# Two fused attention and feed-forward layers: the second layer's norms, projections and row-maximum tiles in another order

## The reference

```python
xn = layernorm(x)
x = x + linear_attention(xn) + ternary_silu_ffn(xn)          # layer 0
xn = layernorm(x)
q, k, v = rope(xn @ q_w.T + q_b), rope(xn @ k_w.T + k_b), xn @ v_w.T + v_b   # 16 heads of 16
attn = softmax(q @ k.T / 4) @ v                              # 1024 x 1024 per head and batch
x = x + attn @ out_w.T + out_b + hadamard_ffn(xn)            # layer 1, hidden size 1024
```

## Time and profile before

| | |
|---|---|
| median of three runs | 838.94 us |
| the profiled execution's own time | 838.99 us |
| its span | 837.2 us |
| busy in the span | PE 762.6 (91%), DVE 533.3 (64%), ACT 430.1 (51%), POOL 290.6 (35%) |
| the stage of layer 1's feed-forward network | 256.40 to 519.75 us, 263.35 us |

### The profile page before, as it was taken

One profiled execution on the slowest core, in us unless ns is written; L12 is line 12 of the kernel. 1 busy time (PEld: TensorE's weight loads), 2 busy tenths in 40 slices (PEclk: granted clock), 3 DMA queues, 4 the chain that ended last, 5 costly groups with the idle time before them and its releaser, 6 DMA issues.

```text
span 837.2 us, 10576 instructions
## 1 busy us (share of the span) xinstructions
PE 762.6 (91%) x3978; PEld 440.7 (53%) x3978; DVE 533.3 (64%) x777; ACT 430.1 (51%) x556; POOL 290.6 (35%) x286
## 2 busy tenths in 40 slices
PE   8767899999999998988988888999999999999896
PEld 6656687876686887655555455333323333333323
DVE  3665546445543433779888887677777777777605
ACT  4324233435454433221111212888887888888793
POOL 0684868635132765541111111021231123122310
PEclk9779999899999999999899999999999999999999
DMA  6127100101000256363111112144333334433211
GB/s 224 51 89 263 52 1 0 51 1 50 1 1 1 68 159 225 102 192 111 61 41 52 50 51 66 52 141 125 95 118 128 108 109 145 142 134 95 76 35 57
DMA packets 25781, 73.72 MB, mean 88 GB/s; under 512 B 4556, under 2 KB 5548, under 8 KB 24772
## 3 DMA queue, kind: packets, MB, share of 16 engines
q1 hardware_dynamic: 21204, 64.97, 23.5%
q0 software_dynamic: 3808, 7.60, 3.1%
q10 hardware_dynamic: 720, 0.48, 0.2%
HBM read 54.15 MB, written 23.06 MB: 92 GB/s over the span
## 4 chain that ended last, share of the span: by engine, by line
PE 66%; DVE 13%; issue 7%; ACT 7%; POOL 6%; DMA 1%; DVEq 0%; POOLq 0%; ACTq 0%
PE PS L663 32%; PE PS L903 13%; PE PS L889 7%; PE PS L872 6%; DVE mx L1137 5%; PE PS L860 4%; ACT P L1334 3%; DVE mx L1145 2%; PE PS L758 1%; POOL ek L1378 1%; POOL XL L1373 1%; POOL zk L1379 1%; PE PS L755 1%; DVE rot L1127 1%; ACT sg L1301 1%
## 5 line engine op out<-in xcount | busy, mean ns | idle before, releaser
L1334 ACT ACTIVATE P<-PS 128x1024 f32<-128x1024 f32 x256 | 248.7, 1024 | 38.9 <-PE PS L889 36.6
L1145 DVE TENSOR_REDUCE mx<-PS 128x1 f32<-128x512 f32 x284 | 182.8, 685 | 68.0 <-PE PS L872 66.8
L1414 POOL TENSOR_TENSOR hl<-sg,hh 128x512 fp32r<-128x512 f32 x64 | 82.1, 1285 | 216.5 <-ACT hh L1308 216.5
L1137 DVE TENSOR_REDUCE mx<-PS 128x2 f32<-128x1024 f32 x114 | 133.3, 1217 | 15.3 <-PE PS L860 15.2
L903 PE MATMUL PS<-P,VV 128*32 128x512 f32 x1024 | 137.0, 607 | 0.5
L889 PE MATMUL PS<-QS,KS 64*128 64x512 f32 x512 | 111.1, 454 | 7.7 <-ACT P L1334 7.1
L1308 ACT ACTIVATE hh<-sg 128x512 fp32r<-128x512 f32 x64 | 40.3, 630 | 133.9 <-DVE sg L1090 92.6
L889 PEld LDWEIGHTS PS<-QS,KS 64*128 64x128 f32 x512 | 48.0, 185 | 86.1 <-ACT P L1334 75.3
L872 PE MATMUL PS<-KM,QM 64*128 64x512 f32 x284 | 67.1, 466 | 6.7 <-DVE mx L1145 6.3
L860 PE MATMUL PS<-KM,QM 64*128 64x512 f32 x228 | 52.3, 491 | 21.2 <-DVE mx L1137 16.5
L872 PEld LDWEIGHTS PS<-KM,QM 64*128 64x128 f32 x284 | 27.6, 185 | 77.3 <-DVE mx L1145 64.2
(11 more groups left out here) (200 smaller groups left out, 1342.7 us busy)
## 6 DMA issues: line engine op xcount, KB each, us to landing
QM<-scr_q SPq DMA_DIRECT2D x16, 512.0 KB, 4.3
KM<-scr_k SPq DMA_DIRECT2D x16, 512.0 KB, 5.3
QS<-scr_q SPq DMA_DIRECT2D x16, 512.0 KB, 4.4
KS<-scr_k SPq DMA_DIRECT2D x16, 512.0 KB, 5.6
scr_q<-spl SPq DMA_DIRECT2D x24, 256.0 KB, 3.0
scr_k<-spl SPq DMA_DIRECT2D x24, 256.0 KB, 3.0
scr_o<-OE POOLq DMA_DIRECT2D x14, 256.0 KB, 2.7
stg<-in_tern SPq DMA_DIRECT2D x3, 1024.0 KB, 4.9
```

Of the source, the lines that this page charges most:

```text
L1137: e.tensor_reduce(mx[p % 2][:, :, qt, half], PS[:, b:b + 2, :], AX.X, ALU.max).then_inc(q["mx"], 2)
L1145: e.tensor_reduce(mx[p % 2][:, h, qt, half:half + 1], bank[b], AX.X, ALU.max).then_inc(q["mx"], 1)
L1334: e.activation(P[s % 4][:, half * 1024:(half + 1) * 1024], PS[:, b:b + 2, :].rearrange("p b n -> p (b n)"), ACT.Exp, scale=0.25).then_inc( ...
L1414: e.tensor_tensor(hl[f % 4][:, :], sg[f % 3][:, :], r32(hh[f % 4][:, :]), ALU.subtract).then_inc(q["hl"], 1)
```

## The change

In layer 1's stage the norms of chunks 2 and 3 no longer come first. The queries and keys of chunks 0 and 1 are projected at once, with two `v` pieces behind each of the four `qk` pieces. The two loads `load_m(0)` and `load_m(1)` follow, and then the norms 6 and 7 one after the other. From there on the side steps are three of two tiles each and one of the remaining projections (`rest`), by turns, until 114 tiles are put. The rates of the weave are other ones. Both late norms now share one pair of tiles, `XCL` and `SQL`; `rstd` lies elsewhere; the first loads wait for six norms in place of eight; and `load_s(1)` stands at the end of the stage.

```diff
-RATE1 = 1.15
-RATE2 = 0.88
+RATE1 = 1.5
+RATE2 = 0.9
@@ def tile
-            if r < 2:
+            if r == 0:
                 put("load_s", r)
@@ def side1
-        def qk(c, n, between, count):
+        def qk(c, n):
             put("qk", c, n, ps.next(), ps.next())
             yield
-            for _ in range(count):
-                between()
+            for _ in range(2):
+                put("v", next(tts), ps.next())
                 yield
             put("qk_split", c, n)
 
-        yield from ln1_pair(2, 3)
         for i in range(4):
             put("ones_v", i)
         for c in (0, 1):
             for n in range(2):
-                yield from qk(c, n, v, 3)
+                yield from qk(c, n)
         put("load_m", 0)
         put("load_m", 1)
-        yield from qk(2, 0, v, 4)
-        yield from qk(2, 1, early, 2)
-        for n in range(2):
-            yield from qk(3, n, early, 3)
+        for n in (6, 7):
+            yield from layernorm(n, ps)
+        rest = chain(*(qk(c, n) for c in (2, 3) for n in range(2)))
+        i = 0
         while len([o for o in order if o[0] == "max"]) < EARLY:
-            early()
+            twice()
             yield
+            i += 1
+            if i % 3 == 0:
+                next(rest, None)
+                yield
+        for _ in rest:
+            pass
 
     sd1 = side1()
     main1 = main(1)
-    weave(islice(main1, 22), sd1, RATE1)
+    weave(islice(main1, 12), sd1, RATE1)
     weave(main1, sd1, RATE2)
     for _ in sd1:
         pass
     put("load_wl")
+    put("load_s", 1)
@@ def program
+        XCL, SQL = (sb(n, kb, [128, 2, 512]) for n, kb in (("XCL", 198), ("SQL", 202)))
         def ln_buffers(n):
             c = n % 4
-            return (XC[c], SQ[c % 2], rstd[c]) if n < 4 else (XC[c % 2], SQ[c % 2 * 2], rstd[c % 2])
+            if n > 5:
+                return XCL, SQL, rstd[c]
+            return (XC[c], SQ[c % 2], rstd[c]) if n < 4 else (XC[c], SQ[2 * c], rstd[c])
@@ vector, ln_mean
                 if n >= 6:
-                    e.wait_ge(q["lnl"], n - 1)
+                    e.wait_ge(q["lnl"], 5 if n == 6 else 7)
```

More of the change, by code:

```diff
@@ L277, in side1, with twice @@
         tts = iter(range(16))
-        def qk(c, n, between, count):
+        def qk(c, n):
             put("qk", c, n, ps.next(), ps.next())
             yield
-            for _ in range(count):
-                between()
+            for _ in range(2):
+                put("v", next(tts), ps.next())
                 yield
             put("qk_split", c, n)
-        def v():
-            put("v", next(tts), ps.next())
-        def early():
+        def twice():
             for _ in range(2):
                 tile(ps, ps)
-        yield from ln1_pair(2, 3)
         for i in range(4):
@@ L429, in program @@
         stg2 = sb("stg2", 190, [128, 2048])
-        rstd = [sb(f"rstd{i}", 202 + i / 32, [128, 4]) for i in range(4)]
+        rstd = [sb(f"rstd{i}", 24.34375 + i / 32, [128, 4]) for i in range(4)]
+        XCL, SQL = (sb(n, kb, [128, 2, 512]) for n, kb in (("XCL", 198), ("SQL", 202)))
         rz = [sb(f"rz{i}", 202.5 + i / 8, [128, 32]) for i in range(2)]
@@ L582, in load_m @@
                 if p == 0:
-                    e.wait_ge(q["lnl"], 8)
+                    e.wait_ge(q["lnl"], 6)
                     e.wait_ge(d["pad"], 32)
@@ L602, in load_s @@
                 e.wait_ge(d[f"m{p % 2}"], slot_value(p))
+                if p == 0:
+                    e.wait_ge(q["lnl"], 8)
                 if p == 1:
@@ L1218, in ln_mean @@
                 if n >= 6:
-                    e.wait_ge(q["lnv"], n - 1)
+                    e.wait_ge(q["lnv"], 5 if n == 6 else 7)
                 e.activation(sq[:, :, :], xc[:, :, :], ACT.Square).then_inc(q["lnq"], 1)
```

## The result

The changed kernel takes 863.67 us, the median of four runs (858.16 to 866.02), against 839.90 (836.48 to 842.00) for the kernel before on the same chip. The ratio is 1.0278, with a 95% interval from 1.0217 to 1.0338: slower by 23.8 us. The prediction had the direction; 863.7 lies 10.7 us above its range. The profiled execution took 863.70 us with a span of 861.9. That span is 24.7 us longer than the one before: 15.2 us in the stage, 4.3 ahead of it and 5.2 behind it. Of the further runs of the kernel before, which stand beside the experiments, one took 2330 us where the others took 835 to 846; it is left out of every ratio and mean.

The account below looks back on a forecast made before the run. PE was taken as the only full engine in chunk 0, with PE and DVE both high but not full in the tile chunks. Terms -4.1 + 6.2 + 0.8 + 1.6 + 2.3 = +6.8 on 838.99 gave 846 us, range 843 to 850.

Parts of the forecast that it names:

- The clock: PE at half clock behind the two `ln_var`: expected twice in place of once, +1.6 us (bounds 0 and 3.2).
- blocks of tiles: The tiles' 57 blocks on PE, priced by what stands ahead of each: 67.5 us against 71.6, so -4.1 us.
- norms' waits: PE's waits at variance and scaling of the two late norms: +6.2 us, bounds 4.7 and 8.5.
- one `v`: One `v` that now stands one piece behind a block waits for its bank: +0.8 us.
- first scores: At the stage's end the last tile, directly ahead, holds the scores' first banks: scores come +2.3 us later.
- loads: Split parts and `load_m(0)` ahead of the first tile, and the late `load_s(1)`: hidden, costed at nothing.
- levelling rival: DVE catches up in every gap, single-piece blocks become short (mean 0.70), clock gains 4 us: 831 us; chance 0.12.
- projections hurt more: Blocks behind four projections among tiles cost 4 us each and drag the next block: +6, 852 us; chance 0.13.
- Same: Norms cost 4.7, the clock nothing more, blocks 0.1 less each: +2 us, 841 us; chance 0.20.
- Wrong: Signs against the forecast: waits for DVE at tiles below 10 us in all, or PE's tile-chunk clock reading 1.00.

Follow-up runs that it names:

- three other traces of before's order: Profiled runs of the kernel before with `rstd` moved (844.16 us), `load_s(1)` late (841.04) or filler elsewhere (846.38); stage 259.9 to 260.0 us, 3.4 lost to the clock.
- second trace of the changed kernel: The changed kernel run again, unedited: 862.08 us, ratio 1.0243 to the kernel before.
- filler run: The changed kernel with unused matmuls, nine ahead of each late `ln_var` and three ahead of each late `ln_scale`: 856.28 us, ratio 1.0173 to the kernel before.
- gap runs: The changed kernel with more pieces between the late norms' steps and rate 1.0 (839.92 us); the same idea with paired norms on own tiles, rate 0.97 (835.77 us).
- its own experiment: The kernel before with `load_s(1)` alone moved to the end of the stage: 841.04 us, ratio 0.9993.
- the pair's kernel: The changed kernel with the two late norms interleaved at the same late place, each on tiles of its own: 853.96 us, ratio 1.0158 to the kernel before.
- the kernel with the rate alone: The changed kernel with `RATE2` 0.97 in place of 0.9 and no other edit: 856.95 us, ratio 1.0197 to the kernel before.

## Why the prediction was wrong

The waits were about right, with one of them too long. The term of the sum that failed is *The clock* (+1.6), and with it "In the tile chunks the mean clock is 0.95 to 0.98; I leave it so": the prediction priced new waits on a full PE as waits alone. The runs showed +8.9 us of clock in the stage in its place, and +14.0 against the three other traces of before's order.

| term | forecast | measured in the profiled stage |
|---|---|---|
| blocks of tiles | -4.1 | -2.6 (69.0 us against 71.6) |
| norms' waits | +6.2 | +4.7 (2.26, 0.66, 1.16, 0.66) |
| one `v` | +0.8 | +0.6 |
| first scores | +2.3 | +2.3 |
| clock | +1.6 | +8.9 |
| loads | 0 | 0 |
| sum | +6.8 | +13.9, of 15.2 |

- *The blocks.* The 30 with a single piece ahead took 1.12 us in mean (forecast 1.06), with the end's wait taken out 1.04; those behind two or more pieces 0.66 each, as forecast; the four behind a projection 0.73, 3.47, 4.29 and 1.16, together 9.65 (9.0); the six with `max_rows` 16.8 (15.5). The levelling rival fell: the mean never came near 0.8. Behind the second and third `qk` the rival "projections hurt more" was right block by block, and wrong as a total. Two of the rivals were added up wrong: from its own terms "Same" comes to +0.7 us and not +2, and four projections at 4 us in place of 2.25 are +7.0 before any block is dragged, not +6.
- *The norms.* First variance 2.26 (1.9 forecast), both scalings 0.66 (0.65), second variance 1.16 (3.0). The last was priced at full clock: at half clock PE itself takes longer over what lies between, and so waits less. In the second trace of the changed kernel, where the clock was full again between the norms (300.2 to 307.0), that wait was 2.15 us. The two terms trade with each other.
- *The clock.* I counted one fall per `ln_var`, 1.6 us in all as before. Measured were 10.2 us at half clock from the end of the first variance's wait on, then 3.4 more, which is 6.8 of the 7.2 us lost in chunk 0; by the same records it was 1.7 before. In chunks 1 to 3 it is 10.2 against 6.8, since the two rotations' waits (2.54 and 3.06) and the four 1.51 us ones of `max_rows` blocks each have 3.4 us at half clock beside or behind them. The prediction read from the earlier trace rows that the fall comes "behind the single-column matmuls". That holds for the 32 records in a row of the order before. The changed kernel has 16 and 16, and the first norm of the filler run and all four norms of the gap runs keep the full clock behind 16: there, idle time ahead of them is what made the difference, and the fall lasted 10.2 us in place of 3.4. That such idle time is followed by half clock also among the tiles is read from the changed kernel's traces; no run took those waits alone away. The rule cited from the Trainium skill (TensorE: Matmul & The Clock Gate, section What's actually happening), that throttled is the default and activity releases it, pointed there: idle waits had to be priced as lost activity as well. The trace agrees with it at 295.5, 367.2 and 408.2 us; at the wait of 2.17 us above, three of four traces show no fall.
- *The signs.* Neither sign of "Wrong" came: the waits at tiles for a reduction were 14.7 us, not below 10, and the clock in the tile chunks fell. The prediction had no sign for a clock lower than before.
- *Loads, end, first tile.* The first tile waited for no load (317.38, in a run of work); `load_s(1)` cost nothing by its own experiment; the end's wait was exact.
- *Outside the stage.* In the profiled runs 4.3 us lie ahead of the stage, where both programs have the same order, and 5.2 behind it; the sum had no term for either. The clock's loss is 4.7 us more ahead of it (23.5 against 18.8) and 3.4 more behind it (5.1 against 1.7), so most of the 9.5 us is again clock. Ahead of the stage the profiled runs of kernels with that same order took 255.7 to 264.0 us, and behind it 317.4 (before) to 326.5. The kernel before was profiled near the lower end of both. How much of these 9.5 us the change causes is open: the clock's mean loss over all runs differs by 14.5 us, and the stage's part of it is 8.9 or 14.0, by which trace of before's order it is held against.

## What to carry to other kernels

On a stage where PE is full, price a new wait of PE twice, once as the wait and once as what the clock may take beside it: here 4.7 us of waits in the norms came with 5.5 us of clock in chunk 0, and in the changed kernel's traces a wait of 2.5 to 3 us for a rotation with 1.7. One trace of the kernel before is not enough to price it: its stage lost 8.5 us to the clock in one run and 3.4 in three others. When a chain such as a norm's is moved, move its cover with it: count the pieces of real work between its steps and put in as many as its hand-overs need before judging the new place. The change was 2.4 to 2.8% slower than the start with one piece or none in the norms' gaps. With one to three, and a higher rate, it was 0.1 to 0.65% faster than the start, and with the norms also paired 0.7%. These runs gained 22 to 28 us over the changed kernel, dummy matmuls 6 to 7. In the early part of this kernel, where PE is not the full engine, a higher PE clock brought 0.7 us at most.

## What the hardware showed that was not expected

- Adding work shortened a stage: 24 matmuls of 0.23 us in the norms' waits, 278.6 to 271.7 us.
- Idle time is not the whole rule. In the pair's kernel a wait of 2.52 us (until 357.73) was followed by no fall, the wait of 2.17 us in before's order had one in one trace of four, and in the kernel with the rate alone the clock fell at 377.7 behind an idle stretch of 0.85 us. Behind 32 matmuls of one column it fell with no wait ahead. What else decides stays open.
- The time ahead of the stage varied by 8 us (255.7 to 264.0) among profiled runs with the same instruction order there, with 17.9 to 29.0 us of clock loss in it.
